# First row pair of an E = M·W product in pieces: chunk order, split low parts and moved codebook steps on one Trainium2 core

## What is computed

```python
x = x + L0_ffn(L0_cond(x))     # L0_cond: x @ w_eff.T, w_eff from a quantized weight with a codebook and a LoRA term
x = x + L1_ffn(L1_cond(x))     # L1_cond: x @ weight.T + bias + low-rank adapter term
# L1_ffn: x @ base_W.T + router (8 experts, top 2) + low-rank expert term
```

## Time and profile before

| | |
|---|---|
| median of 3 runs | 895.06 us (894.72 to 896.3) |
| profiled execution | 895.22 us, its span 893.5 us |
| granted TensorE clock | 1.00 in every stretch |
| TensorE busy | 99% of the span, 4616 matmuls |
| VectorE, ScalarE, GpSimd busy | 76%, 37%, 18% |

### The profile page before, as it was taken

How to read it: one execution, slowest core, us unless ns; L and a number is a source line. 1 busy time by engine, 2 the same in 40 slices (tenths; PEclk the granted TensorE clock), 3 DMA queues, 4 the chain that set the end, 5 groups by cost and what they waited for, 6 DMA issues and landing times.

```text
span 893.5 us, 13665 instructions
## 1 busy us (share of the span) xinstructions
PE 888.1 (99%) x4616; PEld 777.0 (87%) x4616; DVE 679.6 (76%) x1493; ACT 329.6 (37%) x553; POOL 156.7 (18%) x306
## 2 busy tenths in 40 slices
PE   9999999999999999999999999999999999999998
PEld 8999998888998888888888888888888888888887
DVE  6999999786587968889676676776777766767765
ACT  6688878421224433232323223223223223222221
POOL 0210020111001001414202302302302302302300
PEclk9999999999999999999999999999999999999999
DMA  9533340776313042565787887887887886886875
GB/s 347 203 97 121 125 136 25 254 242 200 96 51 95 0 142 85 196 249 205 232 292 253 295 294 248 297 295 247 296 292 251 297 297 244 298 294 245 299 258 205
DMA packets 62403, 192.00 MB, mean 215 GB/s; under 512 B 7905, under 2 KB 12538, under 8 KB 60414
## 3 DMA queue, kind: packets, MB, share of 16 engines
q1 hardware_dynamic: 50460, 158.99, 49.9%
q0 software_dynamic: 11584, 31.87, 12.5%
q10 hardware_dynamic: 290, 0.26, 0.1%
HBM read 158.86 MB, written 32.76 MB: 214 GB/s over the span
## 4 chain that ended last, share of the span: by engine, by line
PE 97%; DMA 1%; SPq 1%; ACT 0%; issue 0%
PE bank L935 30%; PE bank L583 15%; PE bank L584 15%; PE bank L585 15%; PE bank L917 7%; PE bank L903 5%; PE bank L736 2%; PE bank L912 2%; PE bank L1044 2%; DMA lb_raw<-lorabt 1%; PE bank L846 1%; PE bank L863 0%; PE bank L861 0%; PE bank L596 0%; PE bank L594 0%; PE bank L870 0%
## 5 line engine op out<-in xcount | busy, mean ns | idle before, releaser
L935 PE MATMUL bank<-g_hi,xs 128*128 128x512 f32 x440 | 150.1, 398 | 0.0
L554 POOL DMA_DIRECT2D p1sel<-p_scratch x128 | 65.3, 510 | 342.2 <-issue 342.2
L935 PE MATMUL bank<-t_hi,xs 128*128 128x512 f32 x336 | 111.2, 391 | 0.0
L935 PEld LDWEIGHTS bank<-g_hi,xs 128*128 128x128 f32 x440 | 81.7, 188 | 15.3
L935 PE MATMUL bank<-g_lo,xs 128*128 128x512 f32 x220 | 86.8, 394 | 0.0
L1494 DVE TENSOR_TENSOR xs<-x_raw,xs 128x1024 fp32r<-128x1024 f32 x60 | 73.0, 1239 | 12.4 <-ACT xs L1121 11.9
L1121 ACT ACTIVATE xs<-x_raw 128x1024 fp32r<-128x1024 f32 x60 | 61.7, 1053 | 47.1 <-PE bank L935 46.5
L583 PE MATMUL bank<-gx,xs 128*128 128x304 f32 x256 | 78.5, 307 | 0.0
L585 PE MATMUL bank<-gx,xs 128*128 128x304 f32 x256 | 77.4, 302 | 0.0
L584 PE MATMUL bank<-gx,xs 128*128 128x304 f32 x256 | 77.2, 301 | 0.0
L935 PEld LDWEIGHTS bank<-t_hi,xs 128*128 128x128 f32 x336 | 63.1, 188 | 14.0
(11 more groups left out here) (396 smaller groups left out, 2105.9 us busy)
## 6 DMA issues: line engine op xcount, KB each, us to landing
t_hi<-t_scratch SPq DMA_DIRECT2D x82, 512.0 KB, 5.6
t_lo<-t_scratch SPq DMA_DIRECT2D x82, 512.0 KB, 6.6
x_raw<-xq SPq DMA_DIRECT2D x16, 1024.0 KB, 8.0
out<-ost SPq DMA_DIRECT2D x63, 256.0 KB, 7.7
p1sel<-p_scratch POOLq DMA_DIRECT2D x64, 192.0 KB, 5.4
w_raw<-wall SPq DMA_DIRECT2D x15, 512.0 KB, 4.7
w<-e_scratch SPq DMA_DIRECT2D x6, 1024.0 KB, 5.1
ea<-e_scratch POOLq DMA_DIRECT2D x8, 644.0 KB, 5.4
```

The source lines that it names most:

```text
L554: pool.dma_start(f(p1sel[b][STK * s:STK * s + STK, cs]), p1_dram[bass.ds(i * STK, STK), cs]).then_inc(sems[b], 16)
L935: mm = nc.tensor.matmul(bk[j][:], l[:, c, :], m[:, c, :], start=first and c + k == 0, stop=c + k == KH + 1, skip_group_check=True)
```

## The change

- **Loads.** The first piece of chunk 1 is issued ahead of the piece of W's row 1, and chunk 3 comes in two loads as well.
- **ScalarE.** The second piece of chunk 0 is made in two operations (groups 1 and 2). The first piece of chunk 1 comes before the high part of W's row 1. The last operation on the W pair (chunks 4 to 7, 1024 columns in all) becomes two (chunks 4 and 5 after M's chunk 3, chunks 6 and 7 after chunk 4). The eviction `e_out(0, 0)` is moved ahead of the high parts of the LoRA operands.
- **VectorE.** Low parts of chunks 1, 2 and 7 are made in two pieces, that of the W pair's chunks 4 to 7 in two; three small codebook steps move from behind chunk 7 to between the chunks.
- **TensorE.** Chunks 0, 1 and 2 take pieces in a new order, with low parts by piece; chunk 3 takes (0,0) and (1,0) first; chunk 7 does all its high matmuls first, then the low one of (0, 0), then the other three.
- **Positions.** The three codebook steps stand 6 matmuls later each, `DELTA0` 9 matmuls later (from behind chunk 4 of row 1's group 2 to behind chunk 7 of it).
- Counts of `ws_hi` and `ws_lo` rise by one, since there is one more piece; the load of W block 2 waits for `ws_lo` 5 where it waited for 4.

```diff
-DELTA0 = (1, 2, 4)
+DELTA0 = (1, 2, 7)
-CB_AT = {(1, 5): 0, (1, 7): 1, (2, 2): 2}
+CB_AT = {(1, 7): 0, (2, 1): 1, (2, 4): 2}
-M1_HI = (2, 4, 6, 7, 9, 10, 11, 12)
+M1_HI = (3, 5, 7, 9, 11, 12, 13, 14)
+M1_LO = (2, 4, 6, 7, 8, 9, 10, 12)
...
-        ld_part = {0: ld_first, 1: ld_rw0, 2: ld_b0t, 4: st_b}
+        ld_part = {0: ld_first, 1: ld_rw0, 2: ld_b0t, 3: ld_t2, 4: st_b}
...
-                    sp.wait_ge(ws_lo, max(n + 1, 4))
+                    sp.wait_ge(ws_lo, max(n + 2, 5))
...
+            sp.dma_start(m1_raw[1][:, 0:N_FIRST], m1t[P:2 * P, 0:N_FIRST]).then_inc(ld_part[1], 16)
             sp.dma_start(w_raw[1][:, 0:2, :].rearrange("p c n -> p (c n)"), wall[1][:, 0:2 * P]).then_inc(ld_wb, 16)
-            load_first(1)
+            sp.dma_start(m1_raw[1][:, N_FIRST:NM1], m1t[P:2 * P, N_FIRST:NM1]).then_inc(ld_row[1], 16)
...
-            load_m1(3)
+            load_first(3)
...
             pe.wait_ge(m1_hi_s, 1)
             pair_high(0, ALL[0:1])
+            pe.wait_ge(m1_hi_s, 2)
+            pair_high(0, ALL[1:2])
             pair_low(0, ALL[0:1])
             pe.wait_ge(m1_hi_s, M1_HI[0])
-            pair_high(0, ALL[1:3])
+            pair_high(0, ALL[2:3])
             pe.wait_ge(m1_hi_s, M1_HI[1] - 1)
             pair_high(1, ALL[0:1])
             pair_low(0, ALL[1:3])
             pair_high(0, ALL[3:4])
             pair_low(0, ALL[3:4])
+            pair_high(1, ALL[3:4])
+            pair_low(1, (ALL[0], ALL[3]))
             pe.wait_ge(m1_hi_s, M1_HI[1])
-            pair_high(1, ALL[1:4])
-            pair_low(1)
+            pair_high(1, ALL[1:3])
+            pair_low(1, ALL[1:3])
...
             pe.wait_ge(m1_hi_s, M1_HI[KC - 1])
-            for part in (ALL[0:1], ALL[1:3], ALL[3:4]):
-                pair_high(KC - 1, part)
-                pair_low(KC - 1, part)
+            pair_high(KC - 1, ALL)
+            pair_low(KC - 1, ALL[0:1])
+            pair_low(KC - 1, ALL[1:])
...
-                    pair_split(slice(4, KC))
+                    pair_split(slice(4, 6))
+                if c == 4:
+                    pair_split(slice(6, KC))
+            e_out(0, 0)
             act.wait_ge(ld_lora, 32)
             hi_of(la_hi[:], la_raw[:]).then_inc(la_hi_s, 1)
             hi_of(lb_hl[:], lb_raw[:]).then_inc(la_hi_s, 1)
-            for g in range(3):
+            for g in (1, 2):
                 e_out(0, g)
...
-            m1_split(2)
+            m1_split(2, rest)
+            link(nc.vector.tensor_scalar(peak, peak, 1e-8, None, ALU.max))
             m1_split(3)
-            pair_low(4, slice(4, KC))
-            for c in range(4, KC):
+            pair_low(4, slice(4, 6))
+            link(nc.vector.reciprocal(peak, peak))
+            m1_split(4)
+            pair_low(5, slice(6, KC))
+            link(nc.vector.tensor_scalar(cb[:], cb[:], peak, None, ALU.mult))
+            for c in range(5, KC - 1):
                 m1_split(c)
-            link(nc.vector.tensor_scalar(peak, peak, 1e-8, None, ALU.max))
-            link(nc.vector.reciprocal(peak, peak))
-            link(nc.vector.tensor_scalar(cb[:], cb[:], peak, None, ALU.mult))
+            v.wait_ge(m1_hi_s, M1_HI[KC - 1])
+            for cs in (first, rest):
+                lo_of(m1_lo[:, KC - 1, cs], m1_raw[KC - 1][:, cs], m1_hi[:, KC - 1, cs]).then_inc(m1_lo_s, 1)
```

More of the change, by code:

```diff
@@ L620, in pair_high @@
             def pair_high(c, groups):
[L621 to L627, removed]
+                for k, w in enumerate((w_hi, w_lo)):
+                    for row, g in groups:
+                        pe.wait_ge((ws_hi, ws_lo)[k], row + 1 if c < 2 else c // 2 + 2)
+                        n0, n = A_COLS[g]
+                        nc.tensor.matmul(group(row, g)[:, 0:n], w[row][:, c, :], m1_hi[:, c, n0:n0 + n], start=c + k == 0,
+                                         stop=False, skip_group_check=True)
             def pair_low(c, groups=ALL):
-                pe.wait_ge(m1_lo_s, c + 2 if c or groups[0][1] else 1)
+                pe.wait_ge(m1_lo_s, M1_LO[c] - (c in (0, 1, 2, KC - 1) and not any(g for _, g in groups)))
                 for row, g in groups:
@@ L654, in _ @@
                     pair_high(c, (ALL[0], ALL[3]))
+                    if c == 2:
+                        pair_low(c, (ALL[0], ALL[3]))
                     pe.wait_ge(m1_hi_s, M1_HI[c])
@@ L659, in _ @@
                     pair_high(c, ALL)
-                pair_low(c)
+                pair_low(c, ALL[1:3] if c == 2 else ALL)
             pe.wait_ge(m1_hi_s, M1_HI[KC - 1])
-            for part in (ALL[0:1], ALL[1:3], ALL[3:4]):
-                pair_high(KC - 1, part)
-                pair_low(KC - 1, part)
+            pair_high(KC - 1, ALL)
+            pair_low(KC - 1, ALL[0:1])
+            pair_low(KC - 1, ALL[1:])
             for r in range(1, KC + 1):
-                pe.wait_ge(ws_hi, r + 3)
-                pe.wait_ge(ws_lo, r + 3)
+                pe.wait_ge(ws_hi, r + 4)
+                pe.wait_ge(ws_lo, r + 4)
                 for g, (n0, n) in enumerate(A_COLS):
@@ L695, in _ @@
                 for j in range(4):
-                    pe.wait_ge(ws_hi, KC + 4 + j)
-                    pe.wait_ge(ws_lo, KC + 4 + j)
+                    pe.wait_ge(ws_hi, KC + 5 + j)
+                    pe.wait_ge(ws_lo, KC + 5 + j)
                     if j < 2:
@@ L962, in winograd_products @@
                 if not n:
-                    pe.wait_ge(ld_t2, 64)
+                    pe.wait_ge(ld_t2, 16 + 64)
                 product(24, 3, quarter(1, 0, 0), g_quarter(0, 1), False).then_inc(p6_mm, 1)
@@ L1172, in quant_pair @@
                 if t == 0:
-                    act.wait_ge(m1_lo_s, KC + 1)
+                    act.wait_ge(m1_lo_s, M1_LO[KC - 1])
                 if t < 3:
@@ L1198, in _ @@
                     m1_split(c, ld_part[c], slice(0, N_FIRST))
-                    m1_split(c, ld_row[c], slice(N_FIRST, NM1))
-                else:
-                    m1_split(c, ld_row[c], slice(0, NM1))
                 if c == 0:
+                    for g in (1, 2):
+                        m1_split(0, ld_row[0], slice(A_COLS[g][0], sum(A_COLS[g])))
+                    continue
+                if c == 1:
                     act.wait_ge(ld_wb, 16)
                     hi_of(w_hi[1][:, 0:2, :], w_raw[1][:, 0:2, :]).then_inc(ws_hi, 1)
+                m1_split(c, ld_row[c], slice(N_FIRST if c in ld_part else 0, NM1))
                 if c == 1:
@@ L1496, in w_split @@
             def w_split(n):
-                v.wait_ge(ws_hi, n + 3)
+                v.wait_ge(ws_hi, n + 4)
                 lo_of(w_lo[w_set(n)][:], w_raw[n % 2][:], w_hi[w_set(n)][:]).then_inc(ws_lo, 1)
@@ L1509, in m1_split @@
             def m1_split(c, cs=slice(0, NM1)):
-                v.wait_ge(m1_hi_s, M1_HI[c] - (cs.stop < NM1))
+                v.wait_ge(m1_hi_s, 1 if cs.stop < NM1 and not c else M1_HI[c] - (cs.stop < NM1))
                 lo_of(m1_lo[:, c, cs], m1_raw[c][:, cs], m1_hi[:, c, cs]).then_inc(m1_lo_s, 1)
@@ L1544, in _ @@
             mag, peak = vcomp[0:1, :], val0[0:1, 0:1]
+            first, rest = slice(0, N_FIRST), slice(N_FIRST, NM1)
             first_low(0)
-            m1_split(0, slice(0, N_FIRST))
+            m1_split(0, first)
             v.wait_ge(ld_cb, 16)
             link(nc.vector.tensor_scalar(mag, cb[:], -1.0, None, ALU.mult))
-            m1_split(0, slice(N_FIRST, NM1))
+            m1_split(0, rest)
             first_low(1)
+            m1_split(1, first)
             link(nc.vector.tensor_tensor(mag, mag, cb[:], ALU.max))
-            m1_split(1)
+            m1_split(1, rest)
             pair_low(3, slice(2, 4))
+            m1_split(2, first)
             link(nc.vector.reduce_max(peak, mag, AX_X))
-            m1_split(2)
+            m1_split(2, rest)
+            link(nc.vector.tensor_scalar(peak, peak, 1e-8, None, ALU.max))
             m1_split(3)
-            pair_low(4, slice(4, KC))
-            for c in range(4, KC):
+            pair_low(4, slice(4, 6))
[4 more added lines that the diff above has]
+            for c in range(5, KC - 1):
                 m1_split(c)
-            link(nc.vector.tensor_scalar(peak, peak, 1e-8, None, ALU.max))
-            link(nc.vector.reciprocal(peak, peak))
-            link(nc.vector.tensor_scalar(cb[:], cb[:], peak, None, ALU.mult))
+            v.wait_ge(m1_hi_s, M1_HI[KC - 1])
+            for cs in (first, rest):
+                lo_of(m1_lo[:, KC - 1, cs], m1_raw[KC - 1][:, cs], m1_hi[:, KC - 1, cs]).then_inc(m1_lo_s, 1)
             v.wait_ge(ld_pk, 16)
```

## The result

The changed kernel has a median of 896.3 us (895.69 to 897.66, 21 runs) against 895.15 us for the kernel before in the same comparison (894.51 to 896.82, 21 runs). The ratio is 1.0012, 95% interval 1.0007 to 1.0018: slower by 0.6 to 1.6 us, and less than the 0.2% that I had set as the bound of "measurably slower". I had forecast 896.2.

The account below looks back on a forecast made before the run. TensorE, busy for 99% of the span, was taken as the bound. The pair's +0.06 us and the 1.1 us hole at W block 5 sum to +1.16 us, 896.2 us on the median of 895.06; range 894.6 to 897.2.

Parts of the forecast that it names:

- Bound: TensorE, whole run: from 25 us on matmuls stand back to back; only holes before that, about 2.2 us, could be won.
- Chunk 4 takes the pieces' gain back: Row pair: TensorE gets 0.7 us ahead, then waits for chunk 4's low part until 17.05; gain only 0.07 us.
- The second wait that I had forecast, at chunk 5: TensorE waits for chunk 5's low part by 0.06 us, and up to 0.1 us for the restart.
- rival A: Row pair ends 1 us earlier, if chunk 4's low part is there by 16.1: 895.1 us; chance 0.13.
- Handover: Pair to row 1's group 1: two edits trade one lateness for another, 24.67 against 24.61, +0.06 us.
- Position: `DELTA0` 9 matmuls later: dequantization chain 1.64 us later, opening a 1.1 us hole at W block 5.
- B: Rival: the VectorE and ScalarE chain isn't rigid, so no hole at block 5: 895.1 us; chance 0.13.
- C: Rival: pair ends earlier and chain isn't rigid, both together, the only way to be faster: 894.0 us; chance 0.04.
- D: Rival: VectorE becomes the bound of the pair, which ends up to 0.8 us later: 897.0 us; chance 0.12.
- E: Rival: W block 3 late as well, 0.1 us slack left, changes little: 896.3 us; chance 0.58 together with the forecast.
- Size of the hole: TensorE's wait for W block 5's low part at r = 5: 1.00 us, with a restart of 0.1, 1.1 us.
- Sum: Whole run: 0.06 for the pair plus 1.1 for the hole, 1.16 us; 896.2 us on the median.

Follow-up runs that it names:

- b1: Changed kernel with chunk 4's low part made in two pieces as well: 895.92 us, ratio 1.0008 to the kernel before.
- d2: Changed kernel with the loads issued as before and the engines' pieces kept: 895.97 us, ratio 1.0008 to the kernel before.
- c_again: Changed kernel, nothing altered, executed once more for a second profile: 896.96 us.
- a4: Kernel before with only the eviction of (0, 0) moved ahead of the LoRA operands' high parts: 894.51 us, ratio 0.9997; run again, 895.03 us.
- b2: Changed kernel with chunk 7 by groups again, the earlier eviction of (0, 0) kept: 896.18 us, ratio 1.0012 to the kernel before.

## Why the prediction was right

- **Bound.** TensorE is a row nearly without gaps from 25 us on, so the result is a sum of holes. Behind the handover, every experiment's profile moved against that of before at the holes named here and at the late waits and shifts near `t_lo`, and otherwise, once the moved steps are past, by at most 0.1 us.
- **Chunk 4 takes the pieces' gain back.** Forecast: TensorE 0.7 ahead at chunk 4, then held until 17.05, chunk 5 at 17.86. Measured 0.9 ahead, 16.94, 17.74; this execution's loads were 0.2 earlier (chunk 7's high part at 18.87 instead of 19.06). b1 and d2 show that this wait, and no later piece, held the pair. The second wait that I had forecast, at chunk 5, hardly came: its low part was ready at 19.04 and wanted at 19.15. Back to back on VectorE, a piece more costs 0.06 us by starts (0.47 and 0.87 for chunk 7's two, 1.28 for chunk 6's one), less than the 0.09 and 0.15 that I took from rows.
- **A miscount that didn't matter.** Before 10.63 there are 20 matmuls, not 22 (12 of chunk 0 and 8 of chunk 1), so the holes up to there are 1.65 us, not 1.3. The whole, 2.2 us, stays, and the number is in no term of the sum; it makes rival A a little stronger than I had it.
- **Handover.** Forecast +0.06 us for the pair, measured by the distance from chunk 7's high part +0.03 (5.58 - 5.55), and +0.01 in c_again: too small to tell from nothing. a4 and b2 show the trade of the two edits.
- **Position.** Forecast: the dequantization 1.64 later, measured 1.38, since `delta(0)` came at 34.72 and not 34.97, in an execution with earlier loads; relative to TensorE it is 1.54 (1.38 and the 0.16 by which TensorE is ahead), where 1.58 were forecast. The chain is rigid, as assumed. Rivals A to D are excluded: A by 16.88 against 16.1, B and C by the shift of 1.38 at both ends, D by the pair's +0.03. E did not come, and it was as close as forecast: block 3's low part ended at 50.87 (49.65 + 1.22), and its first matmul stood at 51.11, 0.23 behind its neighbour, the usual distance.
- **Size of the hole.** Forecast 1.1, measured 1.03. The release took 0.10 (79.20 to 79.30), not 0.13.
- **Sum.** +1.16 forecast, +1.03 and +0.03 by the holes, +1.15 by the medians, +1.07 by the ratio (0.0012 x 895.15), with an interval of 0.6 to 1.6. That 896.2 and 896.3 lie 0.1 apart is therefore partly luck; what the profiles bear out is the two terms. The profiled execution's span grew by 1.2 by other terms: TensorE's last matmul starts 1.37 later (0.16 less at the handover, 1.0 at r = 5, 0.5 from 687 us on), and behind it 0.2 less follows, 3.4 us instead of 3.6.

What I had too small is the spread. The load-set start of chunk 7's high part ran from 18.67 to 20.06 over 14 profiles, more than the effect itself; the range of 894.6 to 897.2 held the median, but six of the changed kernel's 21 executions lie above it.

## What to carry to other kernels

When a sequence on another engine is released by TensorE's own stream, moving its release later in that stream takes slack from every product that this sequence feeds, however far behind; look for the smallest slack along it (here 0.6 us, 44 us later) before moving it, and move the late product a slot earlier instead. An operand delivered in pieces gains only as far as the piece that is wanted last, here chunk 4's low part. Two edits at one handover should be tried apart: here the earlier eviction alone was worth 0.3 to 0.4 us, and together with "all high first" nothing ("all high first" without the earlier eviction was not run).

## What the runs showed of the hardware that I had not expected

- The load stream at the start isn't equally early in each execution: chunk 7's high part, which its load sets, started between 18.67 and 20.06 us, and the handover moved along: at 24.45 in the changed kernel's first profile, at 25.53 in its second.
- The warm-up matmuls of 388 columns stood 0.32 us apart in both kernels, though the granted clock is shown as 1.00 in that stretch, the level of 2.4 GHz; the working pace of the same shape is 0.176 to 0.18. In the changed kernel's profile the first working matmuls, from 5.83 to 6.80, still had the slow pace; in that of before the last warm-up step was already 0.175. Where the pace changes differs between executions of one kernel, too. In the changed kernel it should have cost nothing (argued, not tested), because TensorE then came to a hole of 0.63 us before chunk 4's low matmuls anyway.
- In the main loop TensorE waits in some executions for a load of `t_lo`, 0.2 to 0.3 us by the view of waits and 0.3 to 0.6 in the position of all that follows, and not in others of the same kernel.
